# Down projection of a fused transformer layer: first weight piece loaded earlier, four tiles' sums kept in SBUF, other tile buffers

## The reference

```python
def layer(x, ...):                       # x: (2, 4096, 2048) fp32
    x = layernorm(x + attention(x))      # 16 query heads, 4 key/value heads, causal, D = 128
    return layernorm(x + ffn(x))

def ffn(x):
    x = fwht(x * SU_ug) / 64                            # Hadamard transform over 2048
    up, gate = x @ W_up.T * s_up, x @ W_gate.T * s_gate # 8192 wide each
    x = fwht(silu(gate) * up * SU_dp) / 64              # Hadamard transform over 8192
    return x @ W_down.T * (Wscale_dp * 64)              # 2048 wide
```

## Time and profile before

| | before |
|---|---|
| median of 3 runs (lowest, highest) | 2091.55 us (2090.55, 2092.16) |
| the profiled execution: time, and span of its slowest core | 2087.97 us, 2086.9 us |
| spans of the eight cores | 2077.2 to 2086.9 us |
| PE busy | 2021.6 us (97%) |
| DVE, ACT, POOL busy | 566.4, 488.4, 149.2 us |
| Wdown pieces: count, size, median from issue to landing | 32, 1024 KB, 10.2 us |

### The profile page before, as it was taken

How to read it: one execution, slowest core, us unless ns; L and a number is a source line. 1 busy time by engine, 2 the same in 40 slices (tenths; PEclk the granted TensorE clock), 3 DMA queues, 4 the chain that set the end, 5 groups by cost and what they waited for, 6 DMA issues and landing times.

```text
span 2086.9 us, 30398 instructions; the slowest of 8 cores (2077.2 to 2086.9 us)
## 1 busy us (share of the span) xinstructions
PE 2021.6 (97%) x11760; PEld 1043.6 (50%) x11760; DVE 566.4 (27%) x1334; ACT 488.4 (23%) x639; POOL 149.2 (7%) x364
## 2 busy tenths in 40 slices
PE   5999999999998999999999999999998999999997
PEld 2444466666665444444444444444444754444456
DVE  0111144445556412212212212122122530303033
ACT  0110088777785101001001001001002410000002
POOL 3000000000000000000000000000000000000001
PEclk9999999999999999999999999999999999999999
DMA  9885133333325355455455455455453743747359
GB/s 153 140 129 94 30 62 77 72 72 73 81 55 92 61 97 98 84 97 97 84 98 96 84 98 96 84 98 94 85 98 79 127 105 70 159 81 156 73 126 311
DMA packets 92812, 207.00 MB, mean 99 GB/s; under 512 B 11776, under 2 KB 51712, under 8 KB 87680
## 3 DMA queue, kind: packets, MB, share of 16 engines
q0 software_dynamic: 34816, 141.74, 39.3%
q1 hardware_dynamic: 57856, 63.32, 10.8%
HBM read 294.31 MB, written 24.12 MB: 153 GB/s over the span
## 4 chain that ended last, share of the span: by engine, by line
PE 88%; DMA 5%; DVE 2%; ACT 2%; issue 1%; POOL 1%; DVEq 0%; SPq 0%; ACTq 0%; POOLq 0%
PE PS L181 88%; DMA AR<-xkv 2%; ACT AR L437 2%; DMA AR<-scr_h 1%; DMA scr_h<-wmt 1%; POOL AR L219 1%; DMA AR<-WdownP 1%; DMA out<-AR 0%; DVE AR L484 0%; DVE AR L451 0%; DMA AR<-AR 0%; DVE AR L371 0%; DVE stat L882 0%; DVE stat L495 0%; DVE AR L528 0%
## 5 line engine op out<-in xcount | busy, mean ns | idle before, releaser
L181 PE MATMUL PS<-AR 128*128 128x512 bf16 (+4 forms) x11296 | 1979.0, 334 | 45.6 <-DMA AR<-WkT 21.0
L181 PEld LDWEIGHTS PS<-AR 128*128 128x128 bf16 x11296 | 1005.0, 98 | 994.5 <-issue 87.3
L437 ACT ACTIVATE AR<-PS,negc 128x1024 bf16<-128x1024 f32 (+7 forms) x384 | 322.8, 865 | 100.3 <-PE PS L181 91.1
L786 ACT ACTIVATE AR<-PS,sgate 128x512 bf16<-128x512 f32 x128 | 88.0, 687 | 825.5 <-PE PS L181 825.5
L790 DVE SCALAR_TENSOR_TENSOR AR<-PS,scombo,AR 128x512 bf16<-128x512 f32 x128 | 96.1, 751 | 445.4 <-ACT AR L786 445.4
L741 DVE CAST AR<-PS 128x512 bf16<-128x512 f32 x128 | 88.5, 692 | 276.0 <-PE PS L181 276.0
L635 POOL DMA_DIRECT2D AR<-WupT x64 | 33.8, 529 | 838.2 <-PE PS L181 838.2
L451 DVE TENSOR_TENSOR AR<-AR,maskb 128x128 bf16<-128x128 bf16 x256 | 52.3, 218 | 117.7 <-ACT AR L437 117.5
L891 DVE TENSOR_TENSOR a_b<-PS,AR 128x512 f32<-128x512 f32 (+1 forms) x16 | 9.7, 622 | 271.5 <-PE PS L181 267.8
L1000 ACT ACT_TABLE_LOAD x1 | 1.3, 1283 | 349.3 <-DVE mv L998 349.3
L276 DVE TENSOR_TENSOR AR<-PS,AR 128x512 bf16<-128x512 f32 x32 | 21.8, 690 | 221.0 <-PE PS L181 221.0
(11 more groups left out here) (72 smaller groups left out, 319.0 us busy)
## 6 DMA issues: line engine op xcount, KB each, us to landing
AR<-WupT POOLq DMA_DIRECT2D x64, 512.0 KB, 6.8
AR<-WgateT POOLq DMA_DIRECT2D x64, 512.0 KB, 11.0
AR<-WdownP POOLq DMA_DIRECT2D x32, 1024.0 KB, 10.2
AR<-AR SPq DMA_DIRECT2D x256, 64.0 KB, 4.9
AR<-xkv POOLq DMA_DIRECT2D x6, 2048.0 KB, 22.1
AR<-WqT POOLq DMA_DIRECT2D x16, 512.0 KB, 6.6
AR<-xtok SPq DMA_DIRECT2D x16, 512.0 KB, 4.3
scr_h<-AR SPq DMA_DIRECT2D x32, 256.0 KB, 2.3
```

The source lines that it names most:

```text
L181: return pe.matmul(o, lhsT, rhs, start=start, stop=stop, skip_group_check=True)
L437: et = p.inc(ac.activation(ebuf[:, :, cs:], sps[:, :, cs:], AF.Exp, bias=negc[:, 0:1], scale=INV_SQRT_D), "ac")
L786: at = p.inc(ac.activation(gsl[k], bank(2 + k), AF.Silu, bias=0.0, scale=sgate[:, c:c + 1]), "ac")
```

## The change

Three edits.

1. `O_WD` is another order of the same six slots. Piece 0 has the middle up/gate slot (c % 3 = 1) and is issued after unit (61, 1), the last user of that slot. Pieces 1 and 2 take the places that 0 and 1 had, at u = 126 and behind the same waits; `ffn_end` issues pieces 3 to 5 only.
2. The last four sums of the fourth chunk (index c = 3, columns 1280 to 1791), for tiles 4 to 7, are not stored to `scr_h2`. They stay in the four `h2` buffers (`kept`); `fetch` brings 256 columns less of the upper half of these tiles, 1280 less 1024 instead of 1792 less 1024, and `final` normalizes the upper half in three instructions with three sources.
3. The buffers `fb` of the last norm: three pairs for tiles 0 to 2 and again for 3 to 5, and two pairs in the first half's storage of `bt` for tiles 6 and 7. The pair in `a_b` and `wmt` is gone. Fetches 0 to 2 are issued ahead of the last chunk, 3 to 5 each after an output of tile 0 to 2, and 6 and 7 after tile 3's matmuls.

```diff
@@ -51,7 +51,7 @@
 O_DG = O_NM + 2 * K1
 assert O_DG + 4 * K1 <= O_WQ
 
-O_WD = [O_T2, O_T2 + 8 * K1, O_XQ, O_XQ + 8 * K1, O_XQ + 16 * K1, O_T2 + 16 * K1]
+O_WD = [O_XQ + 8 * K1, O_T2, O_T2 + 8 * K1, O_XQ, O_XQ + 16 * K1, O_T2 + 16 * K1]
 O_WROW = O_T2 + 24 * K1
 O_HR = O_UN
 O_H2 = O_UN + 4 * K1
@@ -791,9 +791,13 @@
                                                ALU.mult, ALU.mult), "dv")
             free[k] = gsl_free[k] = t_
             pend.append((u, c, hf, t_))
+
+
+            if (c, hf) == (IC - 3, 1):
+                wd_load(0, gt)
             if u == len(order) - 2:
-                wd_load(0, t2A_done, b1_tok[0], b1_tok[1])
-                wd_load(1, t2A_done)
+                wd_load(1, t2A_done, b1_tok[0], b1_tok[1])
+                wd_load(2, t2A_done)
         assert not insert
         ffn_pe = gt
 
@@ -825,7 +829,7 @@
             stage1(*pend.popleft(), acc_free, 4 + n2[0] % 4)
             n2[0] += 1
             end_ffn = [("dv", p.n["dv"]), ("pe", p.n["pe"]), ("ac", p.n["ac"]), *b1_tok]
-            for k in range(2, 6):
+            for k in range(3, 6):
                 wd_load(k, ffn_pe, *b1_tok)
             for k in range(4):
                 hr_load(k)
@@ -915,11 +919,15 @@
         def down_rest(k, dst, tok):
             c, t = outs[k]
             t_ = h2_add(k, dst, tok)
+            if k >= 4 * NT - 4:
+                kept[t] = (dst, h2_stats(t, c, dst, t_))
+                return
             p.w(sy, t_)
             st = p.inc(sy.dma_start(scr_h2[t][:, CH_E[c]:CH_E[c] + CH_W[c]], dst),
                        f"h2s{k % 4}", 16)
             h2_free[k % 4] = [st, h2_stats(t, c, dst, t_)]
 
+        kept = {}
         LAG2, SKEW = 3, 16
         ev = [[None] * IC, [None] * IC]
         late, later, loads = deque(), deque(), deque()
@@ -975,16 +983,16 @@
         stores = [(f"h2s{i}", p.n[f"h2s{i}"]) for i in range(4)]
 
 
-        fb = [(vf(o_, T), vf(o_ + 4 * K1, T)) for o_ in (O_WD[2], O_WD[3], O_WROW)] + \
-            [(a_b[:, :], wmf)]
-        fb += [fb[0], fb[1], fb[2], (vf(0, T), vf(4 * K1, T))]
+        fb = [(vf(o_, T), vf(o_ + 4 * K1, T)) for o_ in (O_WD[2], O_WD[3], O_WROW)]
+        fb += fb + [(vf(o_, T), vf(o_ + 4 * K1, T)) for o_ in (0, 8 * K1)]
         fe_tok, o_tok2 = [None] * NT, [None] * NT
         W3 = CH_E[4]
 
         def fetch(t, *ready):
             p.w(gp, *ready, *stores)
             p.inc(gp.dma_start(fb[t][0], scr_h2[t][:, 0:T]), f"fe{t}", 16)
-            fe_tok[t] = p.inc(gp.dma_start(fb[t][1][:, 0:W3 - T], scr_h2[t][:, T:W3]),
+            w = (CH_E[3] if t in kept else W3) - T
+            fe_tok[t] = p.inc(gp.dma_start(fb[t][1][:, 0:w], scr_h2[t][:, T:T + w]),
                               f"fe{t}", 16)
 
         def final(t, tok, *ready):
@@ -1008,8 +1016,14 @@
             lo = p.inc(ac.activation(lo_, lo_, AF.Identity, bias=nmr2[:, t:t + 1],
                                      scale=r2[:, t:t + 1]), "ac")
             p.w(dv, n_, fe_tok[t])
-            hi = p.inc(dv.tensor_scalar(hi_, hi_, r2[:, t:t + 1], nmr2[:, t:t + 1], ALU.mult,
-                                        ALU.add), "dv")
+            src = [(hi_, 0, T)]
+            if t in kept:
+                w, k_ = CH_E[3] - T, kept[t][0]
+                src = [(hi_[:, 0:w], 0, w), (k_, w, W3 - T), (new, W3 - T, T)]
+                p.w(dv, kept[t][1])
+            for s_, a, b in src:
+                hi = p.inc(dv.tensor_scalar(hi_[:, a:b], s_, r2[:, t:t + 1], nmr2[:, t:t + 1],
+                                            ALU.mult, ALU.add), "dv")
             p.w(sy, hi)
             p.inc(sy.dma_start(out[t][:, T:E], hi_), f"o{t}", 16)
             p.w(sy, lo)
@@ -1018,21 +1032,21 @@
         p.w(dv, wrow_tok)
         row_end = p.inc(dv.tensor_copy(wr4[:, :], wrow[:, W3:E]), "dv")
         p.w(dv, row_end)
-        ready = [wd_free[26], wd_free[27], row_end, None, None, None, None, None]
-        for t in range(4):
+        ready = [wd_free[26], wd_free[27], row_end]
+        for t in range(3):
             fetch(t, ready[t])
         for t in range(NT):
             for f in range(IC):
                 inst = down_mm(4, t, f)
             tok = p.inc(inst, "pe")
-            if t == 3:
-                fetch(7, tok)
-                ready[7] = tok
-            p.w(dv, *stores) if t == 3 else None
             final(t, tok, ready[t])
             if t < 3:
-                ready[t + 4] = o_tok2[t]
-                fetch(t + 4, o_tok2[t])
+                ready.append(o_tok2[t])
+                fetch(t + 3, o_tok2[t])
+            if t == 3:
+                ready += [tok, tok]
+                fetch(6, tok)
+                fetch(7, tok)
         p.w(sy, *o_tok2)
     return nc
```

## The result

| | before | after |
|---|---|---|
| median of the runs beside each other (20 each) | 2091.47 us | 2116.24 us |
| fast runs after / fast runs before, 95% interval | | 1.0076 (1.0044 to 1.0108) |
| profiled execution, span of its slowest core | 2087.97, 2086.9 us | 2116.64, 2115.6 us |
| PE busy on that core | 2021.6 us | 2047.7 us |

The changed kernel is slower, and its times fall in two groups: ten of 15 executions lie at 2114 to 2117 us and five at 2088 to 2091, about where before lies. They answer to the earlier trace rows.

What follows compares the result with a forecast made beforehand. TensorE, busy nearly the whole span, was taken as the bound. Core 0: 2085.2 + 1.8 + 0.25 = 2087.3 us, 0.4 above before; weighing the clock gave -0.2, so a median of 2091.3 us, range 2086.0 to 2094.5.

Steps and rivals of the forecast that it cites:

- Early piece 0: Start of down: first Wdown piece, issued about 28 us before up/gate's end, is there in time; cost nothing.
- The first gap: Start of down: 1.5 us wait for VectorE's evacuation stays, 4.62 us go, clock stays at 2.4 GHz.
- When the pair lands: Sixteen steps into down: last unit's two DMAs land at 1612.6 behind `ws_dp`; TensorE waits 7.1 us on core 7.
- The slow phase behind the long gap: After the wait sixteen steps into down: a slow clock phase again, costing 2.5 us.
- The last norm: Last tiles: core 7 can gain 3.3 us, core 0 nothing; three normalizations in place of one cost +0.25 us.
- The sum: Whole kernel: core 0 becomes slowest at 2087.3 us; weighing the clock gives -0.2 us, a median of 2091.3.
- its two terms: Early first piece: +2.4 us on core 7, +1.8 on core 0; last norm: -3.3 on core 7, +0.25 on both.
- so I count 2.5 us again: Restart after the wait sixteen steps into down: slow clock as before, 2.5 us, now on this side of the point compared.
- the rivals: Pair of DMAs lands early (0.15), clock stays up (0.17), new wait in last tiles (0.06), both gaps slow the clock (0.05).
- the two slower ones: New wait in the last tiles (0.06) or slow clock after both gaps in down (0.05): 2096 us each.
- The range: Whole kernel's median: 2086.0 to 2094.5 us, taking in the clock staying up and stopping short of the slower pair.

Runs made afterwards that it cites:

- p2_only: Changed kernel with Wdown's piece 2 issued with pieces 3 to 5, `ws_dp` left ahead of the last unit's two DMAs: 2084.58 us, 0.9974 of before.
- changed_again: The changed kernel, unaltered, run once more as a control on another chip: 2089.82 us, 1.0000 of before.
- part1_only: Only the early first Wdown piece, on the kernel before, with the last norm as before: 2119.32 us, 1.0061 of before.
- part2_only: Only the kept sums and the other tile buffers, on the kernel before, Wdown's first piece as before: 2088.12 us, 0.9983 of before.
- wsdp_late: Changed kernel with the `ws_dp` load moved behind the last unit's two DMAs and the first four residual loads on SP: 2084.93 us, 0.9971 of before.
- skew28: Changed kernel with the second half's work in the first chunk 28 steps behind the first half's, not 16: 2080.07 us, 0.9957 of before.
- best_b: Changed kernel with the second half 28 steps behind in the first chunk and ScalarE making the first evacuation, second run (first run `best`, 0.9950): 2080.08 us, 0.9955.
- wsdp_late_p2: Changed kernel with `ws_dp` behind the last unit's two DMAs and first four residual loads, and Wdown's piece 2 issued with pieces 3 to 5: 2080.99 us, 0.9953.
- third group: Third chip: changed kernel with short gap filled (1.0002) or pieces 3 to 5 ten steps later (0.9998); `wsdp_late_p2` with a made wait (1.0000); `best` (0.9950).
- the fourth: Fourth chip: the changed kernel again (1.0000), with pieces 3 to 5 ten steps later (1.0004), and with the short gap filled (0.9999).
- the fifth: Fifth chip: the changed kernel a third time (1.0056), with pieces 3 to 5 ten steps later (1.0001), and `best_b` (0.9955).

## Why the prediction was wrong

Forecast 2091.3 us and no change; measured 2116.24, slower.

- **Early piece 0.** Right: issued at 1566.6, no wait for Wdown left.
- **The first gap.** Right: 1.68 us for VectorE's evacuation against 1.5, and the clock stayed at 1.00 behind it.
- **When the pair lands.** Right, and the step on which all else hung: 1612.8, behind `ws_dp` at 1612.5, though issued 5 us earlier. The wait was 7.06 us on core 1. For cores 7 and 0 it was forecast at 7.1 and 6.2 and measured 5.73 and 7.42, with restarts at 1612.55 and 1613.02 (forecast 1612.7 and 1613.7): the landings were right within 0.7 us, the step at which TensorE starts to wait moves by over 1 us from one execution to the next. p2_only corrects the reasoning: it is not the order alone, but the order with Wdown's load beside it.
- **The slow phase behind the long gap.** Right: 0.50 behind it on core 1, from 1613.04 to 1617.2, then 1.00. That costs 2.1 us, half of 4.2, against the 2.5 taken over.
- **The last norm.** Right in kind: all last tiles start 0.1 us after TensorE's end. The three normalizations were mis-sized: from the first one's start to the store's issue 1.27 us against 0.90 for one, so +0.37 and not +0.25; the three took 0.41, 0.54 and 0.41 us, and the 0.28 us counted for 256 columns was the row of a copy, not of a normalization. (`fetch` brings 512 columns less for tiles 4 to 7, 256 in place of 768, and not 256 less.) Edits 2 and 3 alone measured 2 us less (0.9983, 0.9963 to 1.0003), which is not clear of nothing.
- **The sum.** It holds where the stretch is missing: changed_again stands at 1.0000 (0.9991 to 1.0010), where the forecast's -0.2 us is 0.9999, and the five such executions of the first result lie at 2088 to 2091. The halves show its two terms apart: the four executions of part1_only without the stretch have a median of 2092.35, 2.6 us above before's there (2089.8; forecast +2.4 and +1.8), and part2_only lies about 2 us below.
- **What failed** is the sentence "so I count 2.5 us again". It took the price of a gap and restart from the one restart that it read in the trace of before, behind which the clock knew 0.50 and 1.00. Moved sixteen steps on, to a restart released by the landing that also releases 3 MB of loads, a gap of about that length is in about half of the executions on some chips followed by 160 us at 0.81, 26 to 27 us, ten times that price. The runs show that edit 1 brings it (4 of 8 against 0 of 9 for edits 2 and 3), that it is gone on that chip when the gap is shrunk, and that it depends on the chip or the occasion. A slow phase and the three loads on one core of a pair, without the long gap, did not bring it (wsdp_late), and the two cores of a struck pair need not restart together (part1_only). What it takes besides the long gap stays open: the 3 MB of loads at the restart are a hint from nine executions against nine, and why it strikes a pair no run shows. None of the rivals had it, since the prediction had no third level of the clock, and the two slower ones, at +5, were not what happened.
- **The range** took the spread of the clock from two levels and so ended at 2094.5.

The kernels that do bring what edit 1 was able to bring are skew28, best_b and wsdp_late_p2: 0.9957, 0.9955, 0.9953, about 10 us under before and 36 under the changed kernel's first median. ScalarE's first evacuation in best shortened the short gap from 1.7 to 0.7 us and gained nothing that these runs can tell.

## What to carry to other kernels

A transfer that is started earlier helps only up to the next one that is late: find that one's place in its own queue and what runs beside it before counting the gain. Moving a stall was not neutral here though the arithmetic said so: the stretch at 0.81 came with the moved gap and not with the gap in its old place. Cover the wait with work or shorten it. When a time has two groups, compare on one chip, with the control beside it, before crediting an edit.

## What the runs showed of the hardware

The granted clock has a third level in these traces, 0.81, so the two levels named ahead of the prediction are not all. It was held for 160.4 us on cores 0 and 1 of the changed kernel and for 161 us on cores 4 and 5 of part1_only. It began on both cores of a pair within 0.2 us by their own times (1621.6 and 1621.8; 1622.5 and 1622.3), 4.2 to 5.3 us after each core's return from 0.50 to 1.00.

The changed kernel had it in ten of 15 executions in the first result, in 4 of 9 on another chip and in none of ten on a third; part1_only in 4 of 8. The variants with the long gap that ran elsewhere or with the loads delayed never had it: 0 of 29 in the third group, 0 of 15 in the fourth, 0 of 9 in the fifth. The kernel before had it in 1 of 104. A gap of 13.3 us in the middle of chunk 1 did not bring it (0 of 6), on a chip on which the changed kernel was not run.

A wait of 3.1 us already had the clock at 0.50 behind it (wsdp_late, core 4, from 1612.6 to 1616); behind one of 1.7 us it stayed at 1.00.
